# Folding the token transform of an audio tower: even and odd parts, five products per output tile

## The reference, cut to what matters

```python
h = depthwise_conv(x, taps=7) + b_dw            # along the tokens, per channel
h = relu(w_pw @ h + b_pw)                       # 192 x 192 product
h = max over pairs of tokens                    # 1024 -> 512 tokens
y = real(fft2(h))                               # over 512 tokens and 192 channels
y = layernorm(y) * gamma + beta
```

## Time and profile before

| | us |
|---|---|
| median of 3 executions | 518.67 |
| lowest, highest | 516.27, 519.98 |
| the profiled execution | 517.64 |
| its span, first to last instruction | 515.5 |
| PE busy | 410.8 (80%) |
| DVE busy | 279.7 (54%) |
| ACT busy | 159.2 (31%) |
| POOL busy | 81.0 (16%) |

### The profile page before, as it was taken

One profiled execution on the slowest core, in us unless ns is written; L12 is line 12 of the kernel. 1 busy time (PEld: TensorE's weight loads), 2 busy tenths in 40 slices (PEclk: granted clock), 3 DMA queues, 4 the chain that ended last, 5 costly groups with the idle time before them and its releaser, 6 DMA issues.

```text
span 515.5 us, 8094 instructions
## 1 busy us (share of the span) xinstructions
PE 410.8 (80%) x2696; PEld 290.2 (56%) x2697; DVE 279.7 (54%) x842; ACT 159.2 (31%) x299; POOL 81.0 (16%) x120
## 2 busy tenths in 40 slices
PE   3878989798988989888998896404799999997073
PEld 1257746523846238553587265403699999996051
DVE  5976952594885979854251004554043444433483
ACT  0100130284403842048530850200333444342000
POOL 1000000043000510015000330074021222213000
PEclk9978998899999999999995999556799999999565
DMA  7196049700694008900198932043212221230503
GB/s 229 41 325 257 1 114 130 154 2 1 147 145 108 2 16 152 155 16 1 45 151 142 367 123 92 0 152 67 40 38 54 54 53 41 49 80 24 130 0 122
DMA packets 30718, 49.23 MB, mean 95 GB/s; under 512 B 13108, under 2 KB 26932, under 8 KB 28836
## 3 DMA queue, kind: packets, MB, share of 16 engines
q1 hardware_dynamic: 28820, 45.02, 36.9%
q0 software_dynamic: 1872, 3.86, 2.2%
HBM read 38.70 MB, written 12.45 MB: 99 GB/s over the span
## 4 chain that ended last, share of the span: by engine, by line
PE 48%; DVE 22%; DMA 8%; ACT 7%; issue 6%; POOL 5%; SPq 3%; DVEq 0%; POOLq 0%; ACTq 0%
PE att L1312 9%; DVE wide L684 7%; PE ring L1298 7%; PE ring L1094 5%; PE ring L1302 4%; DMA w1b<-k_parts 4%; ACT probs L562 4%; PE ring L1182 4%; PE att L1192 3%; POOL tokens_by_expert L522 3%; PE ring L1113 3%; POOL probs L513 2%; PE misc L1224 2%; PE att L1059 2%; PE ring L1074 1%
## 5 line engine op out<-in xcount | busy, mean ns | idle before, releaser
L513 POOL TENSOR_SCALAR_AFFINE_SELECT probs<-probs 128x256 f32<-128x256 f32 (+1 forms) x72 | 39.2, 549 | 261.4 <-ACT probs L562 261.4
L562 ACT ACTIVATE probs<-ring,ones 128x1024 f32<-128x1024 f32 (+2 forms) x72 | 64.8, 972 | 26.1 <-PE ring L1182 25.9
L684 DVE SCALAR_TENSOR_TENSOR wide<-w,wdw,wide 96x512 f32<-96x512 f32 x90 | 65.8, 797 | 0.2
L1059 PE MATMUL att<-idle 128*128 128x256 bf16 x252 | 36.2, 312 | 23.8 <-DMA tokens_by_expert<-x_all,pos_i 21.9
L1312 PE MATMUL att<-w,probs 128*128 x276 | 49.5, 330 | 0.7 <-DVE probs L910 0.7
L1312 PEld LDWEIGHTS att<-w,probs 128*128 128x128 f32 x276 | 45.0, 193 | 1.1 <-issue 1.0
L1059 PEld LDWEIGHTS att<-idle 128*128 128x128 bf16 x252 | 28.0, 113 | 30.5 <-issue 22.3
L1182 PE MATMUL ring<-w1b 128*128 128x512 bf16 (+3 forms) x192 | 37.2, 310 | 9.9 <-ACT probs L562 6.1
L1192 PE MATMUL att<-probs,va 128*32 128x512 f32 (+3 forms) x384 | 36.7, 445 | 4.8 <-POOL probs L513 3.6
L530 POOL DMA_INDIRECT ffn_by_token<-probs,target x23 | 24.1, 1048 | 97.1 <-DVE probs L917 97.1
L1182 PEld LDWEIGHTS ring<-w1b 128*128 128x128 bf16 x192 | 13.2, 98 | 44.8 <-ACT probs L562 36.4
(11 more groups left out here) (241 smaller groups left out, 639.2 us busy)
## 6 DMA issues: line engine op xcount, KB each, us to landing
w1b<-q_parts SPq DMA_DIRECT2D x32, 192.0 KB, 7.6
w1b<-k_parts SPq DMA_DIRECT2D x8, 576.0 KB, 15.4
w<-in_w SPq DMA_DIRECT2D x1, 4608.0 KB, 14.8
w<-in_x SPq DMA_DIRECT2D x4, 768.0 KB, 11.2
w1a<-in_w1a SPq DMA_DIRECT2D x1, 3072.0 KB, 10.1
q_parts<-q_area SPq DMA_DIRECT2D x24, 96.0 KB, 2.1
k_parts<-k_area SPq DMA_DIRECT2D x24, 96.0 KB, 2.1
tokens_by_expert<-in_empty_rows SPq DMA_DIRECT2D x1, 2231.0 KB, 10.3
```

The source lines that it names most:

```text
L513: nc.gpsimd.affine_select(diag, diag, [[0, len(UNITS[n][1])], [1, P]], ALU.is_ge, minus_one, base=0, channel_multiplier=-1).then_inc(p_rea ...
L562: nc.scalar.activation(squares(n), bank[:, :, 0:N - P * j], ACT.Square, bias=ones[:, 0:1], scale=0.25).then_inc(sq_done, 1)
L684: ins = nc.vector.scalar_tensor_tensor(dst, src, w, dst, ALU.mult, ALU.add)
L1059: nc.tensor.matmul(bank[:, 0:2 * P], idle[:, 0:P], idle[:], start=True, stop=True)
```

## The change

The pooled tokens are folded about token 256 before the transforms. With p(t) the pooled tokens and p(512) = 0, DVE makes even(t) = p(t) + p(512 - t) and odd(t) = p(t) - p(512 - t) for t from 0 to 255, with odd(0) = 0. The channel cosines are then taken of the even part, the channel sines of the odd part, for 2 token tiles and not 4. The token tables keep their first 256 rows. Token 256 has no partner: its channel cosines are made apart (2 products with one weight column, at the end of the second tile) and enter each output tile by one more product, with a single row, whose table (1, -1, 1, ...) is kept in the unused row 0 of the sine table. An output tile takes two cosine products, that one, and two sine products.

A fold needs tokens from both ends, so "half 0" of the convolution, the pointwise product and the pooling now means the outer quarters of the tokens (first and last), "half 1" the inner ones. Operands of 512 contiguous elements become two runs of 256. The release of PE moves from the bias and relu to the even and odd parts, and DVE waits for its own bias and relu ahead of them. ACT copies one tile of 192 columns at a time to `gh`, and ahead of the second the single row of token 256. The two table loads shrink to half (512 KB each). Two small memsets are added at the start of DVE's program.

```diff
-        cos_n = w2[:, 0:NT * N].rearrange("p (i n) -> p i n", n=N)
-        sin_n = w2[:, NT * N:2 * NT * N].rearrange("p (i n) -> p i n", n=N)
+        cos_n = w2[:, 0:NF * N].rearrange("p (i n) -> p i n", n=N)
+        sin_n = w2[:, NF * N:2 * NF * N].rearrange("p (i n) -> p i n", n=N)
...
+        def outer_inner(ap, half):
+            quarters = ap.rearrange("p (q n) -> p q n", q=4)
+            return quarters[:, 1:3, :] if half else quarters[:, 0::3, :]
...
 ACT, front(b)
-                for half in range(2):
-                    act.wait_ge(col_done, 2 * b + half + 1)
+                for i in range(NF):
+                    act.wait_ge(col_done, 2 * b + i + 1)
...
-                    nc.scalar.activation(gh[:, 2 * half:2 * half + 2, :], ring[0][:, half, :].rearrange(
-                        "p (i n) -> p i n", i=2)[:, :, 0:D], ACT.Copy).then_inc(gh_copied, 1)
+                    if i == 1:
+                        nc.scalar.activation(gh[0:1, 0, D:D + NC], ring[0][0:1, i, 2 * P:2 * P + NC], ACT.Copy
+                                             ).then_inc(gh_copied, 1)
+                    nc.scalar.activation(gh[:, i, 0:D], ring[0][:, i, 0:D], ACT.Copy).then_inc(gh_copied, 1)
...
 DVE, convolve(b)
-                            src = xin[:, c, at + tap:at + tap + S // 2]
-                            dst = conv[:, c, at:at + S // 2]
+                            src = outer_inner(xin[:, c, tap:tap + S], half)
+                            dst = outer_inner(conv[:, c, :], half)
...
 DVE, pool(b)
-                        nc.vector.tensor_scalar(pooled[:, o, part], pooled[:, o, part], vec2[:, 1, o:o + 1], 0.0,
-                                                ALU.add, ALU.max).then_inc(pool_done, 1)
+                        part = outer_inner(pooled[:, o, 0:N], half)
+                        st.mark(nc.vector.tensor_scalar(part, part, vec2[:, 1, o:o + 1], 0.0, ALU.add, ALU.max))
+                    st.settle()
...
+                    near, far = pooled[:, :, QT * half:QT * half + QT], pooled[:, :, N - QT * half:N - QT * half - QT:-1]
+                    nc.vector.tensor_tensor(even[:, :, QT * half:QT * half + QT], near, far, ALU.add
+                                            ).then_inc(pool_done, 1)
+                    skip = 1 - half
+                    nc.vector.tensor_tensor(odd[:, :, QT * half + skip:QT * half + QT], near[:, :, skip:],
+                                            far[:, :, skip:], ALU.subtract).then_inc(pool_done, 1)
...
 PE, transform(b)
-                for half in range(2):
-                    pe.wait_ge(pool_done, 4 * b + 2 * half + 2)
-                    for i in (2 * half, 2 * half + 1):
+                for i in range(NF):
+                    pe.wait_ge(pool_done, 2 * (NF * b + i + 1))
+                    for src, dst in ((even, slice(0, NC)), (odd, slice(NC, D))):
                         for c in range(2):
-                            last = nc.tensor.matmul(ring4[0][:, i, 0:D], pooled[:, c, P * i:P * i + P],
-                                                    dft_c[:, c, :], start=(c == 0), stop=(c == 1))
+                            last = nc.tensor.matmul(ring[0][:, i, dst], src[:, c, P * i:P * i + P],
+                                                    dft_c[:, c, dst], start=(c == 0), stop=(c == 1))
+                    if i == 1:
+                        for c in range(2):
+                            last = nc.tensor.matmul(ring[0][0:1, i, 2 * P:2 * P + NC], pooled[:, c, N // 2:N // 2 + 1],
+                                                    dft_c[:, c, 0:NC], start=(c == 0), stop=(c == 1))
                     last.then_inc(col_done, 1)
...
                 for k in range(NT):
-                    for table, dst, src in ((cos_n, slice(0, NC), slice(0, NC)),
-                                            (sin_n, slice(P, P + NS), slice(NC, D))):
-                        for i in range(NT):
-                            last = nc.tensor.matmul(ring4[1][:, k, dst], table[:, i, P * k:P * k + P],
-                                                    gh[:, i, src], start=(i == 0), stop=(i == NT - 1))
+                    cosine, sine = ring4[1][:, k, NS:D], ring4[1][:, k, 0:NS]
+                    for i in range(NF):
+                        nc.tensor.matmul(cosine, cos_n[:, i, P * k:P * k + P], gh[:, i, 0:NC],
+                                         start=(i == 0), stop=False)
+                    nc.tensor.matmul(cosine, sin_n[0:1, 0, P * k:P * k + P], gh[0:1, 0, D:D + NC],
+                                     start=False, stop=True)
+                    for i in range(NF):
+                        last = nc.tensor.matmul(sine, sin_n[:, i, P * k:P * k + P], gh[:, i, NC:D],
+                                                start=(i == 0), stop=(i == NF - 1))
                 last.then_inc(row_done, 1)
```

More of the change, by code:

```diff
@@ L22 @@
 NS = D // 2 - 1
+NF = NT // 2
+QT = N // 4
 HEADS, HD = 12, 16
@@ L130, in build @@
         w2 = sb("w2", [P, E * HC * D])
-        cos_n = w2[:, 0:NT * N].rearrange("p (i n) -> p i n", n=N)
-        sin_n = w2[:, NT * N:2 * NT * N].rearrange("p (i n) -> p i n", n=N)
-        at = 2 * NT * N
+        cos_n = w2[:, 0:NF * N].rearrange("p (i n) -> p i n", n=N)
+        sin_n = w2[:, NF * N:2 * NF * N].rearrange("p (i n) -> p i n", n=N)
+        at = 2 * NF * N
         xin = w2[0:DC, at:at + 2 * (S + 2 * HALO)].rearrange("p (c n) -> p c n", c=2)
         at += 2 * (S + 2 * HALO)
+        even = w2[0:DC, at:at + N].rearrange("p (c n) -> p c n", c=2)
+        odd = w2[0:DC, at + N:at + 2 * N].rearrange("p (c n) -> p c n", c=2)
+        at += 2 * N
         assert at <= E * HC * D
+        def outer_inner(ap, half):
+            quarters = ap.rearrange("p (q n) -> p q n", q=4)
+            return quarters[:, 1:3, :] if half else quarters[:, 0::3, :]
         w1b_area = sb("w1b", [P, E * HID])
@@ L150, in build @@
         conv = wide[0:DC, :].rearrange("p (c n) -> p c n", c=2)
-        pooled = sb("pooled", [DC, 2, N])
-        gh = sb("gh", [P, NT, D])
+        pooled = sb("pooled", [DC, 2, N + 1])
+        gh = sb("gh", [P, NF, D + NC])
         y = sb("y", [P, NT, D])
@@ L547, in front @@
                     act.wait_ge(xn_ready, b)
-                nc.scalar.activation(y[:, :, 0:NC], ring4[1][:, :, 0:NC], ACT.Copy).then_inc(a_copied, 1)
+                nc.scalar.activation(y[:, :, 0:NC], ring4[1][:, :, NS:D], ACT.Copy).then_inc(a_copied, 1)
             def attend(b):
@@ L608, in _ @@
             act.wait_ge(tap_sums_done, 1)
-            nc.scalar.activation(conv[:, 1, S // 2:], att[0][0:DC, :], ACT.Identity,
+            nc.scalar.activation(conv[:, 1, S // 4:3 * S // 4], att[0][0:DC, :], ACT.Identity,
                                  bias=vec2[:, 0, 1:2]).then_inc(tap_sums_copied, 1)
@@ L670, in convolve @@
                 for half in halves:
-                    at = S // 2 * half
                     chunks = 1 if b == 0 and half == 1 else 2
@@ L715, in pool @@
                         dve.wait_ge(col_done, 2 * b)
-                    part = slice(N // 2 * half, N // 2 * half + N // 2)
                     for o in range(2):
-                        pairs = ring[o][0:DC, half, :].rearrange("p (n two) -> p n two", two=2)
-                        st.mark(nc.vector.tensor_reduce(pooled[:, o, part], pairs, AX, ALU.max))
+                        pairs = ring[o][0:DC, half, :].rearrange("p (q n two) -> p q n two", q=2, two=2)
+                        st.mark(nc.vector.tensor_reduce(outer_inner(pooled[:, o, 0:N], half), pairs, AX, ALU.max))
                     for o in range(2):
                         st.settle(but=1 - o)
-                        nc.vector.tensor_scalar(pooled[:, o, part], pooled[:, o, part], vec2[:, 1, o:o + 1], 0.0,
-                                                ALU.add, ALU.max).then_inc(pool_done, 1)
+                        part = outer_inner(pooled[:, o, 0:N], half)
+                        st.mark(nc.vector.tensor_scalar(part, part, vec2[:, 1, o:o + 1], 0.0, ALU.add, ALU.max))
+                    st.settle()
+                    if b > 0:
+                        dve.wait_ge(col_done, 2 * b)
+                    near, far = pooled[:, :, QT * half:QT * half + QT], pooled[:, :, N - QT * half:N - QT * half - QT:-1]
[4 more added lines that the diff above has]
+                                            far[:, :, skip:], ALU.subtract).then_inc(pool_done, 1)
             def untangle(b):
                 dve.wait_ge(a_copied, b + 1)
-                sine = ring4[1][:, :, P:P + NS]
+                sine = ring4[1][:, :, 0:NS]
                 st.then(nc.vector.tensor_tensor(y[:, :, D - 1:NC - 1:-1], y[:, :, 1:NC - 1], sine, ALU.add))
@@ L801, in _ @@
             st.then(nc.vector.memset(nz[:], 0.0))
+            st.mark(nc.vector.memset(pooled[:, :, N:N + 1], 0.0))
+            st.mark(nc.vector.memset(odd[:, :, 0:1], 0.0))
             for m in (xnT, x2T):
@@ L1062, in pointwise @@
                 if b > 0:
```

(12 more changed lines are left out.)

2 lines of the change are left out of this document (1 added, 1 removed).

## The result

The changed kernel takes 529.95 us (median of four executions, 529.45 to 530.90), the kernel before 518.67. The ratio is 1.024, 95% interval 1.020 to 1.028: 2.4% slower, where a gain of about 5 us, to 513.3, was forecast. Some executions of one and the same program take several us longer, at a lower mean clock; the medians include them, the ratios leave them out where they stand well apart. The profiled execution took 529.45 us, its span is 527.6, 12.1 us more than before.

A forecast was written before the change was run, and what follows sets the result against it. TensorE, busy 80% of the span, was taken to bound through the token transform of batches 0, 2 and 3. 517.64 - 2.9 - 2 x (2.33 - 1.5) = 513.1 us, median put at 513.3; range 509.5 to 517.

The forecast's parts named there:

- the clock's: Token transforms of batches 2 and 3: longer gap drops TensorE to 1.2 GHz for part of each, costing 1.5 us each.
- Rival B: Token transform of three batches: shape switches or a lasting clock fall add 2.7 us, giving 516 us; chance 0.15.
- The single-row product: Token transform: eight single-row instructions at 0.115 us each, 0.92 us per batch; bounds 0 and twice that.
- The queue behind: Attention after the token transform: starts when released, at whatever time, so a faster engine triggers nothing else; no term.
- Batch 0: Front of batch 0: wait for `ones` hides DVE's 0.73 us; copies save 0.17 and token products 2.77, together 2.9 us.
- Batch 1: Front of batch 1: the chain goes through the key stack load, so what is saved there is worth nothing.
- DVE: Even and odd parts after bias and relu: TensorE's release 0.73 us later, hidden for the first half, on the path for the second.
- The channel products of the second tile with the single column: Before ACT's copy: eight narrow instructions 0.92 us plus four with one weight column 0.36, together 1.28, 0.29 us less.
- Convolution in two runs: 63 DVE convolution and pooling instructions in the chain, two runs of 256 for one of 512: 0, bound 0.6 us.
- rival D: DVE pays its fixed part once per run, 0.12 us on each of 63 instructions: 7.6 us, giving 520.7 us; chance 0.05.
- Rival A: Clock stays up in batches 2 and 3: 510.1 us, or 511.6 with one of them; chance 0.2.
- Rival C: Saving hidden in batch 2 or 3 by a later key stack or late DVE: 514.6 to 516 us; chance 0.1.

The follow-up runs named there:

- experiment 3: Changed kernel with 16 products of zeros ahead of TensorE's wait for the second tile and 5 ahead of its wait for ACT's copies: 511.86 us, ratio 0.988.
- experiment 4: Kernel before with one single-row product of zeros added to each cosine group of the token transform: 528.36 us, ratio 1.018.
- experiment 6: Changed kernel with the fifth product padded to 128 rows and TensorE's two waits filled with 16 and 5 products of zeros: 509.42 us, ratio 0.987.

## Why the prediction was wrong, point by point

**The step that failed is the clock's**: "priced by the rows at either level: 9.01 - 7.38 = 1.63 us at most, and I take 1.5". That the clock would fall in batches 2 and 3 was right, and the rule of the Trainium skill (TensorE: Matmul & The Clock Gate, section "HAM oscillation"), which names only long gaps, is not borne out: it fell around gaps of 1.66 and 0.54 us, among narrow products. But the price took it that the clock comes back after a while of steady work, as in the rows of before. Between products of 128 rows and of one it does not come back. The transform took 10.8 us and not 4.6 + 1.5. At full clock it takes 6.03 (experiment 3), so 4.8 us of it are the clock's (in batch 3, with 10.3 us, 4.3). The bound of 1.63 us fell even without the alternation: with padded rows the transform took 8.0 us unfilled and 4.70 filled, 3.3 us for the clock, since it came back later than in the rows of before. Rival B named this ("the second fall of the clock is not over after one stretch"), with a price of 2.7 us in all and a chance of 0.15; the three transforms that count took about 13 us more than forecast, five times that.

**The single-row product.** I took 0.115 us per instruction with twice that as the upper bound, 1.84 us for the eight instructions. In the changed kernel they stand apart, as the last paragraph of the prediction asked: the successor of a pair starts 0.66 us behind it (157.74 to 158.40), where an ordinary pair at 0.50 takes 0.42. At full clock the four products cost 2.23 us (experiment 4), above the bound: 0.33 us for each excursion to another height and back. No row of before showed one, and no run stood behind the bound of "twice an ordinary instruction". The 128-row products were right: 4.70 us for 40 (experiment 6) against 4.6.

**The queue behind.** "That a faster engine triggers nothing else" looked only at gains. With the clock down, the 16 zeros ahead of the attention last 3.35 us in place of 1.91 and end behind `y_done` (169.32). This adds 1.0 us in batch 2. In batch 3 the clock was still at 0.50 in the first scores, and zeros and scores add 1.6 us. In batch 2 the sum is 0.9 + 3.4 + 1.0 = 5.3 of the 5.4 us: later start of the transform, its longer time, the start of the attention. In batch 3 it is 0.8 + 2.9 + 1.6 = 5.3 us.

**Batch 0.** Forecast -2.9 us, measured +2.0. ACT's wait for `ones` hid the fold's delay there, as said (the transform starts at 34.66, 34.48 before); the transform is 1.8 us longer for the reason above. My assumption that the low-clock stretch stays as it was failed.

**Batch 1.** Worth nothing, as forecast, but by luck: the next attention starts 2.0 us late, what batch 0 had brought. The expected saving was a loss, its transform ends 4.6 us later and the zeros 5.9, and the 3.31 us of cover took up most of that. The zeros, not the key load, now end last there.

**DVE.** +0.73 us was forecast for the release, 0.91 measured: from pointwise half 1 to the second tile's products 6.48 us (148.06 to 154.54) after 5.57 before (145.96 to 151.53). The even and odd parts took the 0.42 and 0.41 us forecast; the bias pair grew from 0.60 to 0.72. The first half is hidden, as said. The channel products of the second tile with the single column brought no saving: 1.59 us to ACT's copy against 1.61, where 0.29 was forecast. The eight took 1.06 us (154.54 to 155.60) where 0.92 was forecast, the four 0.49 where 0.36 was. That 0.09 us for one of the four was also a slip: half of 0.196 is 0.098. ACT's copies cost nothing extra, as forecast (0.51 to 0.54 us before and after).

**Convolution in two runs** costs nothing: 12 instructions take 7.96 us in both kernels, which settles rival D. The smaller tables bring nothing: the first load takes 6.57 us, 6.35 before. Rival A (the clock stays up) did not arise by itself; with the gaps filled the time was 511.9 us, 1.8 above its 510.1, with the alternation in it. In the sum of the chances A and the forecast give 0.46 to faster, not 0.47; nothing hangs on it. Rival C did not arise; no key load ends late in batches 2 and 3.

## What to carry to other kernels

Count a matmul by its neighbours: a product with few rows between products of 128 rows costs extra (0.33 us here at full clock, there and back), and a row of such alternations can hold a fallen clock down for as long as it lasts (10.8 and 17.5 us here). Pad it with zeros to the neighbours' height, or issue all such products together. When an edit cuts TensorE work but puts it behind a longer wait, fill the wait with products that nobody needs before judging the edit. Here padding alone brought 2.4% slower to no difference, the fill alone to 1.2% faster, both to 1.3% faster (0.8 to 1.8).

## What was not expected of the hardware

- Products of 1 and of 32 rows cost the same among 128-row ones, 6.03 us a transform, and 96 rows cost what 128 cost, 4.70 us.
- Single-row products that follow one another cost 0.25 us an instruction at 1.2 GHz, near the 0.21 to 0.25 of others.
- With TensorE busy without a break the granted clock stayed at 0.50 for 17 us (experiment 4, batch 1), while in the same execution the same instructions ran 9.6 us at 1.00 when they had started there. So the busy share alone does not tell the granted clock; in the same work it hung on the level at which the work began.
